# Another order of the last stage's steps in a graph and expert kernel: logits four rows in front, expert layer between turns, scores spread first

## What is computed

```
def _L1_gnn_ref(inputs, adj, H_v):
    scores = jnp.squeeze(inputs @ H_v, -1)
    mask = adj != 0.0
    logits = jnp.where(mask, adj * scores[None, :], neg)
    m = jnp.max(logits, axis=1, keepdims=True)
    e = jnp.where(mask, jnp.exp(logits - m), 0.0)
    s = jnp.sum(e, axis=1, keepdims=True)
    return (e / jnp.where(s > 0, s, 1.0)) @ inputs

def _L1_ffn_ref(x, router_w, router_b, W1, b1, W2, b2):
    idx = jnp.argmax(xf @ router_w.T + router_b, axis=-1)
    h = jax.nn.relu(xf @ W1[idx] + b1[idx])
    return jax.nn.relu(h @ W2[idx] + b2[idx])
...
x = x + _L1_gnn_ref(_layernorm(x), adj, H_v)
x = x + _L1_ffn_ref(_layernorm(x)[None], ...)[0]
```

## Time and profile before

| what | us |
|---|---|
| median of 3 runs (3163.5 to 3173.11) | 3163.86 |
| the profiled execution | 3170.45 |
| its span | 3168.7 |
| PE busy | 2133.7 |
| POOL busy | 1993.4 |
| DVE busy | 1764.0 |
| ACT busy | 1038.7 |

### The profile page before, as it was taken

The page is one execution under the profiler, slowest core; times in us unless marked ns, Lnnn a source line. Parts: engine busy times, 40 slices in busy tenths (PEclk is TensorE's granted clock), DMA queues, the critical chain, the costliest instruction groups (busy, mean ns, idle before and its releaser), DMA issues.

```text
span 3168.7 us, 41159 instructions
## 1 busy us (share of the span) xinstructions
PE 2133.7 (67%) x13440; PEld 1420.2 (45%) x13498; DVE 1764.0 (56%) x6187; ACT 1038.7 (33%) x1971; POOL 1993.4 (63%) x2075
## 2 busy tenths in 40 slices
PE   5255565657565667676777778686878776774768
PEld 3134343434343444453554546454646554443333
DVE  3636564746565656566565747565656655336441
ACT  3133232323232324233333434242434322323333
POOL 0056777777777777777777777767776777770000
PEclk8667686868687979788888879798989888886889
DMA  2023434343434344444444443434343434353200
GB/s 59 16 81 105 134 111 137 112 136 114 136 114 137 112 134 117 122 126 125 126 124 128 123 124 104 139 101 137 102 122 100 118 110 118 115 173 102 76 17 7
DMA packets 172565, 348.15 MB, mean 110 GB/s; under 512 B 38816, under 2 KB 93760, under 8 KB 170176
## 3 DMA queue, kind: packets, MB, share of 16 engines
q0 software_dynamic: 98304, 268.57, 29.4%
q1 hardware_dynamic: 71408, 71.71, 7.1%
q10 hardware_dynamic: 2640, 5.24, 0.5%
HBM read 333.83 MB, written 11.53 MB: 109 GB/s over the span
## 4 chain that ended last, share of the span: by engine, by line
POOL 36%; PE 24%; DVE 16%; issue 14%; ACT 6%; DMA 2%; DVEq 2%; SPq 0%; ACTq 0%; POOLq 0%
POOL ring L736 36%; PE acc L815 7%; PE wide L924 3%; PE turn L806 3%; DVE kv L1307 2%; DMA ring<-in_kv_table,idxT 2%; PE acc L406 2%; PE rowsum L787 1%; PE wide L868 1%; PE wide L440 1%; DVE att_m L1335 1%; ACT att_p L1087 1%; ACT pt_sb L1032 1%; PE wide L867 1%; DVE pos L1378 1%
## 5 line engine op out<-in xcount | busy, mean ns | idle before, releaser
L736 POOL DMA_INDIRECT ring<-in_kv_table,idxT x2048 | 1985.9, 970 | 854.6 <-issue 607.8
L815 PE MATMUL acc<-kv,pt_sb 128*128 128x128 f32 x3968 | 597.5, 304 | 116.6 <-ACT pt_sb L1032 116.1
L787 PE MATMUL rowsum<-ring,w_block 128*32 128x256 f32 x4096 | 349.3, 443 | 405.0 <-DMA ring<-in_kv_table,idxT 399.8
L815 PEld LDWEIGHTS acc<-kv,pt_sb 128*128 128x128 f32 x3968 | 541.4, 213 | 163.3 <-ACT pt_sb L1032 163.3
L1032 ACT ACTIVATE pt_sb<-turn 128x512 f32<-128x512 f32 (+3 forms) x544 | 291.2, 558 | 349.9 <-PE turn L806 348.2
L787 PEld LDWEIGHTS rowsum<-ring,w_block 128*32 128x32 f32 x4096 | 101.1, 116 | 615.7 <-DMA ring<-in_kv_table,idxT 452.0
L924 PE MATMUL wide<-kv,qT 128*128 128x512 f32 (+3 forms) x576 | 267.5, 599 | 108.0 <-DVE gs L1307 83.4
L1335 DVE TENSOR_REDUCE att_m<-wide 128x1 f32<-128x128 f32 (+14 forms) x120 | 147.0, 1225 | 182.9 <-PE wide L924 177.5
L1307 DVE CUSTOM_DVE_ANT_0 kv<-wide,att_p 128x2048 f32<-128x2048 f32 x56 | 128.3, 2291 | 213.5 <-ACT att_p L1087 209.1
L806 PE MATMUL turn<-ident,att_p 128*128 128x128 f32 x960 | 163.2, 306 | 84.6 <-ACT kv L1049 70.8
L924 PEld LDWEIGHTS wide<-kv,qT 128*128 128x128 f32 x576 | 112.1, 212 | 239.4 <-issue 238.5
(11 more groups left out here) (245 smaller groups left out, 3079.0 us busy)
## 6 DMA issues: line engine op xcount, KB each, us to landing
ring<-in_kv_table,idxT POOLq DMA_INDIRECT x2048
kv<-in_adj SPq DMA_DIRECT2D x27, 1024.0 KB, 5.3
wq_pair<-in_Wq SPq DMA_DIRECT2D x64, 128.0 KB
v_dram<-sums_sb SPq DMA_DIRECT2D x128, 64.0 KB
kv<-v_dram SPq DMA_DIRECT2D x16, 512.0 KB
att_p<-in_Wo SPq DMA_DIRECT2D x16, 512.0 KB, 5.4
kv<-in_adj ACTq DMA_DIRECT2D x5, 1024.0 KB, 7.8
x_dram<-x SPq DMA_DIRECT2D x17, 64.0 KB, 1.9
```

Of the source, the lines that this page charges most:

```text
L736: pool.indirect_dma_start(ring[:, slot, i, :], None, kv_table, bass.IndirectOffsetOnAxis(idxT[:, r % 2, u:u + 1], 0))\
L787: mm = pe.matmul(rowsum[32 * k:32 * k + 32, 0:ROW], w_block[:, at:at + 32], ring[:, slot, k, :], start=(tk == 0), stop=(tk == 3))
L815: mm = pe.matmul(dst, pt_sb[:, q % 2, b * P:(b + 1) * P], rhs(4 * q + b), start=(q + b == 0), stop=(q == len(widths) - 1 and b == widths[q ...
```

## The change

`plan_last` no longer follows the rule; it writes the order out. The exponentials get a letter of their own, E. Rows 4 to 7 have logits and exponentials ahead of the first sum. In a round of the loop the order is now A, two turns of the next round, B, then logits of the round after that between the third and fourth turn and behind, C, and H, Y and Z of the same round ahead of the next sum. The third round has no H; the last one starts with its sum and then does H2, B3, Y2, C3, Z2, H3, Y3, Z3. `output` turns back into `rowsum` instead of `wide`, and waits are adapted: the waits of `route` go, the transposes back of `sum_rows` wait for the latest final addition shown, those of `output` for the one of a round ago. In the last round's `end` item PE's spread of the scores and ACT's copy of it stand ahead of the first pair.

```
         def plan_last():
...
             last = T // 4 - 1
+            order = [("E", 0), ("E", 1), ("T", 0), ("E", 2), ("T", 1), ("L", 4), ("E", 3), ("T", 2), ("L", 5), ("T", 3), ("L", 6),
+                     ("L", 7), ("E", 4), ("E", 5), ("E", 6), ("E", 7)]
+            for u in range(last):
+                r = 4 * u + 4
+                order += [("A", u), ("T", r), ("T", r + 1), ("B", u)]
+                if u < last - 1:
+                    order += [("L", r + 4), ("T", r + 2), ("C", u), ("L", r + 5), ("T", r + 3), ("E", r + 4), ("H", u),
+                              ("L", r + 6), ("E", r + 5), ("L", r + 7), ("E", r + 6), ("Y", u), ("Z", u), ("E", r + 7)]
+                else:
+                    order += [("T", r + 2), ("C", u), ("T", r + 3)]
+            return order + [("A", last), ("H", last - 1), ("B", last), ("Y", last - 1), ("C", last), ("Z", last - 1),
+                            ("H", last), ("Y", last), ("Z", last)]
...
-            def sum_rows(u):
+            def sum_rows(u, shown):
...
                 after(pe, x3_made, u)
+                after(pe, moe_out, shown)
...
             def route(u):
...
-                after(pe, moe_relu, u)
...
-                after(pe, moe_out, u)
...
             def output(u):
...
                 pe.wait_ge(moe_relu, u + 1)
+                after(pe, moe_out, u)
                 for j in range(4):
-                    mm = pe.transpose(wide[:, 1536 + j * P:1536 + (j + 1) * P], y_T[:, j * P:(j + 1) * P], ident[:, :])
+                    mm = pe.transpose(rowsum[:, j * P:(j + 1) * P], y_T[:, j * P:(j + 1) * P], ident[:, :])
...
+                if it["last"]:
+                    show_scores(0, T - 4, 1)
                 fetch(it["fetch"][0])
...
                 fetch(it["fetch"][1])
-                if it["last"]:
-                    show_scores(0, T - 4, 1)
                 fetch(it["fetch"][2])
```

More of the change, by code:

```diff
@@ L312, in plan_last @@
         def plan_last():
-            order = []
-            for i in range(T + 1):
-                u, place = i // 4 - 1, i % 4
-                if i < T:
-                    order.append(("L", i))
-                if u >= 0 and place == 2:
-                    order.append(("B", u))
-                if u >= 0 and place == 3:
-                    order.append(("C", u))
-                if u >= 1 and place == 0 and i < T:
-                    order.append(("H", u - 1))
-                if u >= 1 and place == 1:
-                    order += [("Y", u - 1), ("Z", u - 1)]
-                if i > 0:
-                    order.append(("T", i - 1))
-                if u >= 0 and place == 0:
-                    order.append(("A", u))
-            last = T // 4 - 1
-            return order + [("H", last - 1), ("Y", last - 1), ("B", last), ("Z", last - 1), ("C", last), ("H", last),
-                            ("Y", last), ("Z", last)]
+            last = T // 4 - 1
+            order = [("E", 0), ("E", 1), ("T", 0), ("E", 2), ("T", 1), ("L", 4), ("E", 3), ("T", 2), ("L", 5), ("T", 3), ("L", 6),
[10 more added lines that the diff above has]
+                            ("H", last), ("Y", last), ("Z", last)]
         last_order = plan_last()
@@ L449, in output @@
                 pe.wait_ge(moe_relu, u + 1)
+                after(pe, moe_out, u)
                 for j in range(4):
-                    mm = pe.transpose(wide[:, 1536 + j * P:1536 + (j + 1) * P], y_T[:, j * P:(j + 1) * P], ident[:, :])
+                    mm = pe.transpose(rowsum[:, j * P:(j + 1) * P], y_T[:, j * P:(j + 1) * P], ident[:, :])
                 mm.then_inc(moe_back, 1)
+            shown = 0
             for stage, i in last_order:
@@ L457, in tail_tensor @@
                 elif stage == "A":
-                    sum_rows(i)
+                    sum_rows(i, shown)
                 elif stage == "B":
@@ L466, in tail_tensor @@
                     output(i)
+                    shown = i + 1
         def tail_scalar(act):
@@ L475, in tail_scalar @@
             for stage, i in last_order:
-                if stage == "L":
+                if stage == "E":
                     act.wait_ge(mix_logit, logits_done(i))
@@ L585, in tail_vector @@
             for stage, i in last_order:
-                if stage == "L" and i >= FIRST:
+                if stage == "L":
                     logits(i)
@@ L594, in tail_vector @@
                     after(dve, t_out[i % 2], 16 * (i // 2))
-                    dve.tensor_tensor(y_moe[i % 2], wide[:, 1536:2048].rearrange("p (j n) -> p j n", j=4), x3[i % 2],
+                    dve.tensor_tensor(y_moe[i % 2], rowsum[:, :].rearrange("p (j n) -> p j n", j=4), x3[i % 2],
                                       ALU.add).then_inc(moe_out, 1)
@@ L1176, in end @@
                     load_row(act, 4)
+                    act.wait_ge(score_shown, 1)
+                    act.activation(score_b[:, 0:1536], wide[:, 0:1536], ACT.Copy).then_inc(score_in, 1)
                 fetch(it["fetch"][0])
@@ L1179, in end @@
                 fetch(it["fetch"][1])
-                if it["last"]:
-                    act.wait_ge(score_shown, 1)
-                    act.activation(score_b[:, 0:1536], wide[:, 0:1536], ACT.Copy).then_inc(score_in, 1)
                 fetch(it["fetch"][2])
```

## The result

The changed kernel takes 3121.11 us (median of 4 runs, 3112.82 to 3131.2) against 3163.68 for the kernel before (4 runs, 3161.24 to 3173.11). The ratio of the runs is 0.9849, 95% interval 0.9828 to 0.987; the quotient of the two medians, 0.9865, lies inside that interval. A second measurement on another occasion gave 3120.63 (6 runs) against 3170.92 (17 runs), ratio 0.9838 (0.9808 to 0.9869). By the ratios the gain is 48 to 51 us; the first pair of medians alone gives 42.6.

What follows compares the result with a forecast made beforehand. DVE's chain was taken to bound the last round's end, PE the tail, where it idles for 57 of 248.8 us. Gains 9.6 + 1.3 + 31.4 = 42.3 us: profiled 3128, median 3122, range 3107 to 3140.

Steps and rivals of the forecast that it cites:

- Spread: End of last round: PE's score-spreading transposes moved forward let DVE start 10.2 us sooner; gain 9.6 us, bounds 5 and 10.2.
- POOL may issue its last gathers late, by 0.5 us, or by 2: End of last round: a pair consumed 3.2 us later delays POOL 0.5 us, or 2 with transposes at 1.2 GHz.
- DVE still ends last: Mask of own keys: PE has the own scores by 2854.5 to 2856; DVE comes for them at 2859.
- the spread gains less: Rival, end of last round: POOL's delay makes own scores come last, half of 9.6 us goes; 3127 us, chance 0.06.
- First rows: Before the first sum: one ACT exponential moves behind the fourth row's copies; gain 1.3 us, bounds 0 and 2.
- The new order at full clock: Tail: the four rounds from the first sum, laid out at full clock, take 200.4 us against 248.8.
- Surcharge of a low clock: Tail: 17 us added for low PE clock, bounds 2.3 and 41; a third of 24 chunks behind holes taken as low.
- the clock stays up: Rival, tail: PE's longest hole falls from 12 to 3.4 us, hidden layers at full clock; surcharge 5, 3110 us, chance 0.22.
- The residual's long waits: Tail: PE's two waits of about 12 us for the residual's normalised rows, 23.8 together, fall to 1.1 each.
- Hidden layers low throughout: Rival, tail: transposes don't hold the clock, each loop hidden layer runs low; surcharge 32, 3137 us, chance 0.20.
- Not running ahead: Rival, tail: logits come later than ACT's exponential, so rectifiers and hidden layer wait; about 3150 us, chance 0.04.
- slower: Rival, tail: PE falls to 1.2 GHz in the first hole and gaps keep it there; 3215 us, chance 0.03.

Runs made afterwards that it cites:

- the holes filled: The changed kernel with extra PE products, unused, ahead of the route's products and of the first rounds' one-hot transposes; 3122.65 us in one run.
- the far logits by kind: The changed kernel with DVE's far logits of the first four rows as four masks, then four products, then four maxima; 3119.01 us in one run.

## Why the prediction was right, and where it was not

The time came out as forecast, 3121 against 3122, and so did the sign. The sum did not come out term by term: two terms were off in opposite directions, and the profiles give 51.5 us where the sum had 42.3. That the median still met 3122 so closely is luck: the forecast gain was 6 to 9 us too small, going by the ratios, and it was taken off a median of three runs that lies 7 us below that of the later 17 runs of the kernel before.

**Spread: 9.6 forecast, 6.7 measured.** PE's and ACT's parts were right (2.84 us for the spread, 3.2 assumed; DVE starts at once). The step that failed is "POOL may issue its last gathers late, by 0.5 us, or by 2". It was 5.9. The step looked at the ring slot that PE frees later, where POOL paused 0.40 us instead of 0.30, and charged the work side by side to DVE alone, though the row it rested on, DVE's 1.84 us beside POOL in the earlier trace rows, showed the two beside each other. So "DVE still ends last" fell, and the rival "the spread gains less" has the right mechanism; its 4.8 us less are 2.9. In the one trace with 30.76 us the gain is 4.5: POOL's gathers fell otherwise against DVE's passes there, the one at the first mask took 1.77 us instead of 0.94, and POOL ended 18.4 us behind DVE's first pass instead of 16.0.

A gather beside a mask ends 0.11 us behind it (2837.25 + 2.01 against 2837.93 + 1.22). The Trainium skill (SBUF — State Buffer, "SBUF: two separate sides") says that a DVE pass in a mode with two ports, or one with two inputs in SBUF (this only against a GpSimd instruction that reads SBUF), and a GpSimd instruction exclude each other over a shared port pair, and that GpSimd can't write the descriptors of its transfers while a pass in such a mode holds the pair. The rows agree for the masks. For products they agree only in part: the gather at 2833.55 (1.56 us) ended at 2835.11, in the midst of a product that ran from 2834.37 to 2836.13.

**First rows: 1.3 forecast, 1.25 measured.** In six traces of the new order the first exponential lies 19.7 to 20.4 us ahead of the first sum, in four of the old order 21.0 to 21.5.

**The new order at full clock: 200.4 us forecast.** With the holes filled the four rounds took 54.5, 54.7, 30.9 and 62.4, where the layout had 54.4, 54.4, 31.0 and 60.6. The last round's 1.8 is the output of the third round's expert layer, 8.83 us instead of 7.13 in every trace of the new order but one (the far logits by kind, 7.13). The waits were near the layout: 1.8 for the residual (1.1), 0.7 for the first rectifier (0.5).

**Surcharge of a low clock: 17 forecast, 4.6 measured** (2.9 by the filled holes and 1.7 of that output; 205.3 - 200.4 is 4.9). This is the term that was mis-sized, and the tail came out as the rival "the clock stays up" had it, with a surcharge of 5, though not for the rival's reason, the shorter hole: with a hole of 12 us kept, the old order too ran a hidden layer at full clock once the exponential stood behind the rectifiers. The step that failed is "of the 24 chunks that follow such holes I take a third as low, since the old first three rounds were low for 32 to 44%". None of the 64 product parts of the hidden layers was low: they took 35.7 us in sum. In the loop's hidden layers the old low chunks did not follow the hole ahead of the layer; they followed a wait of 2 us for ACT in the third chunk, which the exponential in front of the rectifiers caused. That exponential had itself waited 1.15 us for DVE's logits, while the changed kernel's starts at once. PE and ACT in the trace of before, then ACT in that of the changed kernel:

```profile
2958.62 1.46 PE L440 MATMUL wide<-qT,att_p 128*128 128x512 f32 x2 [1.97 <-ACT ring L504]
...
2960.54 2.08 PE L440 MATMUL wide<-qT,att_p 128*128 128x512 f32 x2
```

```profile
2955.90 2.00 ACT L478 ACTIVATE kv<-kv,mix_nm 128x2048 f32<-128x2048 f32 x1 [1.15 <-DVE mix_nm L539]
```

```profile
2939.28 1.99 ACT L475 ACTIVATE kv<-kv,mix_nm 128x2048 f32<-128x2048 f32 x1
```

The rows of before stood in the trace. The prediction used the share of low time by round and did not look up where in the round it lies. It named rectifiers behind an exponential as something that would make it wrong, and gave that wait 0.5 us; the new order is right because of just that. The first sum, too, lost its 2.3 us: it takes 14.00.

A wait of 2 us is not the whole account of the clock. In the changed kernel it is 0.50 between 3078 and 3080, inside the output that takes 8.83 us, though PE had waited at most 0.69 us at a time since the sum's start at 3047.25; and in the last hidden layer of the old order two chunks were low, or five, behind the same waits ahead of the layer. What brings the clock down there stays open.

**The residual's long waits.** They went as forecast, but the reason was told incompletely. "DVE has logits, one row or two, between the sum and that residual" is what stood there last; DVE had been idle for 37.56 us before, at the addition that waits for PE's output behind the sum. The logits two rows ahead with the output in its new place already take the long waits away.

**The rivals.** Hidden layers low throughout (3137) did not come. Ahead of the layer shown above PE ran only transposes, 1.04 us for four (0.6 at full clock, give 0.66) and 3.26 for sixteen (3.75 where the third row is low), and the first chunk runs at full speed at once. The granted clock is 0.50 from 2936 to 2937, 0.80 in the next microsecond and 1.00 from 2938 on, so it rose to 2.4 GHz while transposes ran. The rule of the Trainium skill that the prediction named (TensorE: Matmul & The Clock Gate, Part 4: PE-mode transpose) would have had it stay low; this trace speaks against it. Not running ahead (3150) and slower (3215) did not come either.

**What was to show it.** The sums stand 55.2 and 54.7 us apart, then 33.2, against 55 to 62 (the second a little below it) and 31 to 36; the residual's wait is 1.9 at most; no chunk is at 2.5, no later sum above 16. The mask came 6.7 us earlier instead of 10, with the own scores later than DVE: the sign that was named for a wrong spread term, and it was wrong.

## What to carry to other kernels

Ask of a low clock where in the round it lies and what wait stands in front of it: here a wait of 2 us in the middle of dense products cost another 1.5 to 4.7 us behind it, while filling holes of 12 us ahead of a stage gained nothing that the scatter let see. Before a difference of a few microseconds in a stretch is called an effect, look for a second trace of the same stretch: the old tail differed by 3.4 us from itself. When an engine in order waits, look at what it is standing in front of and what is queued behind that; with one waiting addition put elsewhere, DVE stands still around the second sum for 6.56 and 14.00 us instead of 37.56. Before moving DVE work beside POOL's gathers, price the gathers too, not only the DVE passes.

## What the runs showed of the hardware

An indirect gather of POOL took 0.95 us with DVE idle and 1.4 to 2.2 us beside DVE's passes: about one gather per product of 1.76 us, one per two masks of 1.22. The other way round, two masks took 4.14 us instead of 2.4 beside a memset and a selection on POOL.

With products in every hole the granted clock of three rounds rose from 0.91, 0.94 and 0.90 to 1.00, and the rounds became shorter by 0.6, 0.0 and 2.3 us: in the second, where the time stayed, PE would have waited for the one-hot anyway.

The granted clock rose from 0.50 to 1.00 while PE ran nothing but transposes (2936 to 2938), and it fell behind waits of 2.0 to 2.8 us in the middle of dense products, in all eight hidden layers with such a wait, in four traces.
